# Cross attention: context halves made during self-attention and kept in DRAM; query halves split once per 128-row tile and laid over the partitions by transfers inside SBUF

## The reference, cut to what matters

```python
def _L0_xattn_ref(q, k, v, gamma):          # q is x, k and v are ctx_2048: (4, 512, 512)
    h = 8                                    # heads, each of dq = 512 // 8 = 64 rows
    qh = q.reshape(B, h, dq, Lq)
    kh = k.reshape(B, h, dq, Lk)
    vh = v.reshape(B, h, dv, Lk)
    scale = 1.0 / jnp.sqrt(jnp.asarray(dq, dtype=q.dtype))
    qk = jnp.einsum('bhdq,bhdl->bhql', qh, kh) * scale
    sm = jax.nn.softmax(qk, axis=-1)
    ret = jnp.einsum('bhql,bhdl->bhdq', sm, vh)
    return gamma * ret.reshape(B, Dv, Lq)
x = _layernorm(x + _L0_attn_ref(x, W_K, W_Q, W_V, W_O))
x = _layernorm(x + _L0_xattn_ref(x, ctx_2048, ctx_2048, gamma))
x = _layernorm(x + _L0_ffn_ref(x, W_g, W_u, W_d))
```

## Time and profile before

| | |
|---|---|
| median of 3 runs | 1504.17 us (1502.49 to 1505.21) |
| the profiled execution | 1502.57 us, of which the span is 1500.8 us |
| self-attention | from 0 to the barrier at about 992 us |
| cross attention | about 993 to 1238 us |
| feed-forward | the rest |
| busy over the span | PE 96%, DVE 73%, ACT 48%, POOL 42% |

### The profile page before, as it was taken

How to read it: one execution, slowest core, us unless ns; L and a number is a source line. 1 busy time by engine, 2 the same in 40 slices (tenths; PEclk the granted TensorE clock), 3 DMA queues, 4 the chain that set the end, 5 groups by cost and what they waited for, 6 DMA issues and landing times. The chain is left out here.

```text
span 1500.8 us, 24088 instructions
## 1 busy us (share of the span) xinstructions
PE 1434.7 (96%) x6988; PEld 1146.6 (76%) x7008; DVE 1100.5 (73%) x2368; ACT 725.1 (48%) x1549; POOL 636.6 (42%) x493
## 2 busy tenths in 40 slices
PE   7999999999999999999999999859999989999996
PEld 5788888888888888888888888737887765565564
DVE  4667677776777676777767776678999995796854
ACT  3444444545444444444353544438987863323332
POOL 1333424334243334242433433357887853343432
PEclk9999999999999999999999999979999999999998
DMA  6566666666656666666666664811224103000000
GB/s 175 155 166 169 167 169 163 167 161 166 161 164 160 161 161 171 167 165 164 162 167 158 168 166 133 210 50 54 60 60 151 36 1 112 1 29 28 0 29 28
DMA packets 193609, 185.09 MB, mean 123 GB/s; under 512 B 97057, under 2 KB 170785, under 8 KB 193313
## 3 DMA queue, kind: packets, MB, share of 16 engines
q1 hardware_dynamic: 192416, 184.09, 45.7%
q10 hardware_dynamic: 1152, 0.52, 0.2%
HBM read 113.25 MB, written 71.30 MB: 123 GB/s over the span
## 5 line engine op out<-in xcount | busy, mean ns | idle before, releaser
L583 ACT ACTIVATE probs<-probs,neg_max 128x128 f32<-128x128 f32 (+3 forms) x256 | 142.5, 557 | 357.8 <-DVE neg_max L707 350.2
L411 POOL TENSOR_TENSOR v_lo<-placed,v_hi 128x512 fp32r<-128x512 f32 x64 | 83.2, 1299 | 366.1 <-ACT v_hi L589 366.1
L413 POOL TENSOR_TENSOR pT_lo<-placed,pT_hi 128x1280 fp32r<-128x1280 f32 x64 | 189.2, 2956 | 0.0
L767 DVE SCALAR_TENSOR_TENSOR acc<-attn_bank,prob_recip,acc 128x512 f32<-128x512 f32 x256 | 174.8, 745 | 8.1 <-PE attn_bank L483 3.3
L1303 POOL TENSOR_TENSOR prod_lo<-prod,prod_hi 128x512 fp32r<-128x512 f32 x64 | 84.7, 1323 | 143.2 <-ACT prod_hi L1412 143.2
L707 DVE CUSTOM_DVE_ANT_0 probs<-attn_bank,mask 128x128 f32<-128x128 f32 (+3 forms) x256 | 117.2, 481 | 8.3
L682 DVE TENSOR_TENSOR qT_lo<-attn_bank,qT_hi 128x512 fp32r<-128x512 f32 x64 | 44.2, 691 | 105.2 <-ACT qT_hi L571 105.2
L950 POOL TENSOR_SCALAR xprobs<-xprobs,xprob_recip 128x512 f32<-128x512 f32 x128 | 99.9, 797 | 36.1 <-DVE xprob_recip L1130 36.0
L719 DVE STREAM_TRANSPOSE turned<-probs 128x256 f32<-128x256 f32 (+1 forms) x384 | 113.9, 362 | 0.0
L1362 PE MATMUL y_bank<-wdT_f32r,prod_hi 128*128 128x512 f32 x256 | 110.7, 432 | 2.3 <-POOL prod_lo L1303 1.8
L483 PE MATMUL attn_bank<-woT_hi,zT_hi 128*128 128x512 f32 x256 | 101.2, 395 | 8.9 <-DVE zT_lo L682 8.9
(11 more groups left out here) (145 smaller groups left out, 3887.5 us busy)
## 6 DMA issues: line engine op xcount, KB each, us to landing
turned_scratch<-turned SPq DMA_DIRECT2D x64, 896.0 KB, 3.9
placed<-turned_scratch SPq DMA_DIRECT2D x256, 224.0 KB, 4.3
rows_twice<-in_ctx_dram SPq DMA_DIRECT2D x64, 128.0 KB, 2.6
acc<-in_x_dram SPq DMA_DIRECT2D x16, 256.0 KB, 5.2
rows<-in_L_attn_W_V_dram SPq DMA_DIRECT2D x64, 64.0 KB, 2.3
rows<-in_L_attn_W_O_dram SPq DMA_DIRECT2D x64, 64.0 KB, 2.7
rows_twice<-in_L_ffn_W_g_dram SPq DMA_DIRECT2D x64, 64.0 KB, 3.1
rows_twice<-in_L_ffn_W_u_dram SPq DMA_DIRECT2D x64, 64.0 KB, 2.0
```

The costliest lines, as they stand in the source:

```text
L413: nc.gpsimd.tensor_tensor(pT[par][1][:], placed_probs, pT[par][0][:].bitcast(F32), ALU.subtract).then_inc(p_lo, 1)
L583: nc.scalar.activation(probs[:, cols], probs[:, cols], ACT.Exp, bias=low[:, par, t:t + 1], scale=-1.0, accum_out=total[:, par, t:t + 1]).t ...
L767: nc.vector.scalar_tensor_tensor(out=acc[:, b * NT + t, :], in0=s_bank[t][:], scalar=recip[:, b, t:t + 1], in1=acc[:, b * NT + t, :], op0= ...
```

## The change

Four things are done.

1. In self-attention, once for each of its 16 heads, SP loads one 128-row tile of the context (`load_split_tile`) into slot 1 of the buffer (now `rows_pair`), between the use of this slot for wu and the next load of wu. POOL scales it by 1/8 and splits it with three instructions (`split`), SP writes the halves (512 KB) to DRAM (`keep_halves`). The load of wu moves from the loads of b = 0 to those of b = 1, behind a wait for the split.
2. At the end of self-attention the last such split stands on POOL between the last `halves_lo` and the two `norm_gpsimd`, and SP waits for the last write before the barrier.
3. In cross attention POOL no longer splits context rows. SP loads hi and lo ready-made from DRAM straight into `cp`, as two transfers of 256 KB (`load_halves`), four items ahead instead of six, when the scores of item m + 2 are done.
4. x is split once for a pair of items: ACT rounds the whole 128-row tile (half as many instructions, of twice the partitions), POOL subtracts (one instruction per pair), and SP copies each head's hi and lo from there to the two halves of `xs` with two transfers of 128 KB inside SBUF for each item. DVE's instruction (L1136) is gone.

The diff, cut to its core:

```diff
 class ContextRows:
+    def load_split_tile(self, sp, n):
+        sp.dma_start(self.pair[:, 1, :], self.tiles[:, bass.ds(n, 1), :].rearrange("p o d -> p (o d)")).then_inc(self.split_loaded, 16)
+    def split(self, nc, pool, halves, k, n):
+        raw = self.pair[:, 1, :]
+        if not isinstance(n, int) or n > 0:
+            pool.wait_ge(self.halves_kept, n * 16)
+        wait_apart(pool, k, self.split_loaded, n * 16 + 16)
+        nc.gpsimd.tensor_scalar(raw, raw, XSCALE, 1.0, ALU.mult, ALU.mult).then_inc(self.scaled, 1)
+        wait_apart(pool, k, self.scaled, n + 1)
+        nc.gpsimd.tensor_scalar(halves[:, 0, :], raw, 1.0, 1.0, ALU.mult, ALU.mult).then_inc(self.split_hi, 1)
+        wait_apart(pool, k, self.split_hi, n + 1)
+        nc.gpsimd.tensor_tensor(halves[:, 1, :], raw, halves[:, 0, :].bitcast(F32), ALU.subtract).then_inc(self.split_done, 1)
+    def keep_halves(self, sp, halves, k, n):
+        wait_apart(sp, k, self.split_done, n + 2)
+        sp.dma_start(self.kept_tiles[:, bass.ds(n, 1), :, :].rearrange("p o k d -> p (o k) d"), halves[:].bitcast(F32)).then_inc(self.halves_kept, 16)
+    def load_halves(self, sp, cp, b, h):
+        for side in range(2):
+            sp.dma_start(cp[h % 2][side * XD:(side + 1) * XD, :, :],
+                         self.kept[bass.ds(b, 1), h * XD:(h + 1) * XD, :, :].rearrange("o r k d -> (o r) k d")).then_inc(self.halves_loaded[h % 2], 16)
...
 attention, sync: loads(h, b, more)
                     if b == 0:
                         wait_apart(sp, k, f_turn, h * 3 + 1)
                         load_gate_up(sp, "wg", h)
+                    if b == 1:
+                        wait_apart(sp, k, rows.split_done, h + 1)
                         load_gate_up(sp, "wu", h)
...
                     if b == 3:
                         keep_signs(h, 0)
+                        wait_apart(sp, k, f_turn, h * 3 + 3)
+                        rows.load_split_tile(sp, h)
...
                         keep_signs(h, 1)
                         keep_signs(h, 2)
+                        rows.keep_halves(sp, halves, k, h)
...
                 exchange(FIRST + 2, 0)
+                loads(H - 1, 1, False)
                 loads(H - 1, 2, False)
                 keep_signs(H - 1, 0)
                 exchange(FIRST + 3, 1)
+                sp.wait_ge(f_turn, (H - 1) * 3 + 3)
+                rows.load_split_tile(sp, H - 1)
...
+                rows.keep_halves(sp, halves, k, H - 1)
+                sp.wait_ge(rows.halves_kept, H * 16)
 attention, gpsimd
                 for b in range(1, B):
                     halves_lo(FIRST + b, b % 2)
+                rows.split(nc, pool, halves, k, H - 1)
                 for b in range(2):
                     norm_gpsimd(nc, pool, norm, k.minus_half, b)
 cross_attention, sync
-                    nb, nh = ahead(b, h, 6)
-                    if exists(m + 6, ITEMS) and exists(m + 4, ITEMS):
-                        wait_count(sp, cp_ready, m + 5)
-                        source.load_twice(sp, nb, nh)
+                    nb, nh = ahead(b, h, 4)
+                    if exists(m + 4, ITEMS):
+                        if exists(m + 2, ITEMS):
+                            wait_apart(sp, k, scores_full, m * NT + 3 * NT)
+                        source.load_halves(sp, cp, nb, nh)
+                        rows = slice(nh % 2 * XD, (nh % 2 + 1) * XD)
+                        if nh % 2 == 0:
+                            wait_apart(sp, k, x_lo, nb * PAIRS + (nh // 2 + 1))
+                        for part in range(2):
+                            sp.dma_start(xs[nh % 2][part * XD:(part + 1) * XD, :].bitcast(F32),
+                                         x_parts[rows, part, :]).then_inc(xs_loaded[nh % 2], 16)
                     if is_item(b, h, B - 2, 0):
                         signs.load(sp)
 cross_attention, gpsimd
-                    if exists(m + 4, ITEMS):
-                        if exists(m + 2, ITEMS):
-                            wait_apart(pool, k, scores_full, m * NT + 3 * NT)
-                        split_context(*ahead(b, h, 4))
+                    if h % 2 == 0 and exists(m + 4, ITEMS):
+                        nb, nh = ahead(b, h, 4)
+                        wait_apart(pool, k, x_hi, nb * PAIRS + (nh // 2 + 1))
+                        tile = acc[:, bass.ds(nb * NT + nh // 2, 1), :].rearrange("p o d -> p (o d)")
+                        nc.gpsimd.tensor_tensor(x_parts[:, 1, :].bitcast(F32R), tile, x_parts[:, 0, :], ALU.subtract).then_inc(x_lo, 1)
 cross_attention, tensor
                     if t == 0:
-                        pe.wait_ge(cp_ready, nb * XH + (nh + 1))
-                        pe.wait_ge(x_lo, nb * XH + (nh + 1))
+                        pe.wait_ge(source.halves_loaded[nh % 2], nb * (32 * PAIRS) + 32 * (nh // 2 + 1))
+                        pe.wait_ge(xs_loaded[nh % 2], nb * (32 * PAIRS) + 32 * (nh // 2 + 1))
 cross_attention, scalar
-                        if j == 2 and exists(m + 4, ITEMS):
+                        if j == 1 and h % 2 == 0 and exists(m + 4, ITEMS):
                             nb, nh = ahead(b, h, 4)
-                            rows = slice(nh % 2 * XD, (nh % 2 + 1) * XD)
-                            if exists(m + 2, ITEMS):
-                                act.wait_ge(scores_full, m * NT + 3 * NT)
-                            nc.scalar.activation(xs[nh % 2][rows, :], acc[rows, bass.ds(nb * NT + nh // 2, 1), :].rearrange("p o d -> p (o d)"),
-                                                 ACT.Copy, scale=XSCALE).then_inc(x_hi, 1)
+                            for i in range(2):
+                                wait_count(act, xs_loaded[i], nb * (32 * PAIRS) + 32 * (nh // 2))
+                            nc.scalar.copy(x_parts[:, 0, :].bitcast(F32R),
+                                           acc[:, bass.ds(nb * NT + nh // 2, 1), :].rearrange("p o d -> p (o d)")).then_inc(x_hi, 1)
 cross_attention, vector
-                        if j == 2 and exists(m + 4, ITEMS):
...
-                            nc.vector.scalar_tensor_tensor(out=xs[nh % 2][other, :], in0=acc[rows, bass.ds(nb * NT + nh // 2, 1), :].rearrange("p o d -> p (o d)"),
-                                                           scalar=XSCALE, in1=xs[nh % 2][rows, :].bitcast(F32),
-                                                           op0=ALU.mult, op1=ALU.subtract).then_inc(x_lo, 1)
```

More of the change, by code:

```diff
@@ L33 @@
 SCALE = 1.0 / math.sqrt(DH)
+XSCALE = 1.0 / math.sqrt(XD)
 MASKED = -1.0e10
@@ L91, in __init__ @@
         self.tiles = context.rearrange("b (t p) d -> p (b t) d", p=P)
+        self.kept = nc.dram_tensor("context_halves", (B, S, 2, D), F32).ap()
+        self.kept_tiles = self.kept.rearrange("b (t p) k d -> p (b t) k d", p=P)
         self.nat = [sb(f"rows{t}", [P, D]) for t in range(NT)]
-        self.twice = sb("rows_twice", [P, 2, D])
+        self.pair = sb("rows_pair", [P, 2, D])
         self.gamma = sb("gamma", [P, 1])
         self.nat_loaded = [sem(f"ctx_loaded{t}") for t in range(NT)]
-        self.twice_loaded = [sem(f"ctx_twice_loaded{i}") for i in range(2)]
+        self.split_loaded = sem("ctx_split_loaded")
+        self.scaled, self.split_hi, self.split_done = sem("ctx_scaled"), sem("ctx_hi"), sem("ctx_split")
+        self.halves_kept = sem("ctx_halves_kept")
+        self.halves_loaded = [sem(f"ctx_halves_loaded{i}") for i in range(2)]
         self.gamma_loaded = sem("gamma_loaded")
@@ L100, in load_tile @@
         sp.dma_start(self.nat[t][:], self.tiles[:, bass.ds(b * NT + t, 1), :].rearrange("p o d -> p (o d)")).then_inc(self.nat_loaded[t], 16)
-    def load_twice(self, sp, b, h):
-        for half in range(2):
-            sp.dma_start(self.twice[half * XD:(half + 1) * XD, h % 2, :],
-                         self.context[bass.ds(b, 1), h * XD:(h + 1) * XD, :].rearrange("o r d -> (o r) d")).then_inc(self.twice_loaded[h % 2], 16)
+    def load_split_tile(self, sp, n):
[17 more added lines that the diff above has]
+                         self.kept[bass.ds(b, 1), h * XD:(h + 1) * XD, :, :].rearrange("o r k d -> (o r) k d")).then_inc(self.halves_loaded[h % 2], 16)
     def load_gamma(self, sp):
@@ L234, in attention @@
         f_turned = sb("f_turned", [P, D])
-        raw_ffn = rows.twice
+        raw_ffn = rows.pair
+        halves = sb("ctx_halves", [P, 2, D], F32R)
         sign_gu = [sb(f"sign_{n}", [P, NC, P], BF16) for n in ("g", "u")]
@@ L382, in _ @@
                     rows.load_tile(sp, 0, t)
-                sp.wait_ge(f_turn, H * 3 + 1)
-                for h in range(2):
-                    rows.load_twice(sp, 0, h)
                 rows.load_gamma(sp)
+                rows.keep_halves(sp, halves, k, H - 1)
+                sp.wait_ge(rows.halves_kept, H * 16)
             def by_chunk(x):
@@ L427, in step @@
                         weight_lo("wq", h + 2)
+                    if b == 3:
+                        rows.split(nc, pool, halves, k, h)
                 with pool.Fori(0, H - 1) as h:
@@ L732, in _ @@
```

(9 more changed lines are left out.)

18 lines of the change are left out of this document (3 added, 15 removed).

## The result

The changed kernel takes 1511.56 us (median of 6 runs, 1509.62 to 1512.9), the kernel before 1503.76 (6 runs, 1502.32 to 1505.21). The ratio is 1.0052, with a 95% interval of 1.0039 to 1.0064: slower by some 7.8 us. My sum gave +3.7 on the profiled execution, and the forecast was 1507.1. The profiled execution took 1511.56 us, with a span of 1509.7 against 1500.8 before, so 8.9 us are to be found in the traces.

A forecast was written before the change was run, and what follows sets the result against it. PE was taken to set the pace, except at cross attention's start, items 16 to 18 and 24 to 28. +3.2 + 2.0 + 2.1 - 3.6 = +3.7 on 1502.57 gave 1506.3, raised to 1507.1; range 1500.5 to 1513.5.

The forecast's parts named there:

- the late chain: Rival in steady cross attention: query transfers land too late in each pair, 6.3 us above the sum, 1513.4; chance 0.14.
- The loop of self-attention, nothing: Self-attention's loop: POOL's 2.7 us of new instructions fit its idle time and PE never waits, so no change.
- The end of self-attention, +3.2: End of self-attention: the last split delays DVE, PE and the barrier by 2.7 us, the last exchange adds 0.5.
- The start of cross attention, +2.0: Start of cross attention: the query tile's chain delays the first score by 3.2 us, DVE's relief takes off 1.2.
- Steady cross attention, nothing: Steady pairs of cross attention: query transfers land before PE needs them and DVE's relief gains nothing, so no change.
- Items 16 to 18, +2.1: Cross attention's sign loads: item 21's transfers wait behind them and PE stalls, +2.1 us where DVE's relief alone gives -2.6.
- Items 24 to 28, -3.6: Late cross attention, where DVE is the limit: four removed instructions and faster norm work save 3.6 us.
- the signs block nothing: Rival at cross attention's sign loads: no transfer is held behind them, sum -1.0, 1502.4 us; chance 0.20.
- the query chain late in each pair: Rival in steady cross attention: SBUF transfers land in 4.3 us, PE stands 0.45 per pair, 1513.4 us; chance 0.14.
- a wait inside the loop: Rival in self-attention's loop: SP's wait or POOL's split delays each round, 1522 us at 1 us each; chance 0.04.
- DVE's relief pays in more of the stage: Rival in cross attention: DVE's relief shortens the stage by 10 us, sum -3.6, 1499.8 us; chance 0.16.
- The sign that I gave as right: Profile sign: one PE wait on a context or query transfer, 3 to 4 us, near item 18 and nowhere else.

The follow-up runs named there:

- all partitions: Changed kernel with the same context and query bytes in as many transfers, each laid over 128 SBUF partitions instead of 64: 1509.85 us, ratio 1.0040.
- Engine queries: Changed kernel with ACT and DVE making the query halves for each item as before, context halves still loaded from DRAM: 1512.67 us, ratio 1.0058.
- signs late: Changed kernel with the load of all kept signs (4 MB) moved from item 16 to item 28: 1502.83 us, ratio 0.9998.

## Why the prediction came out as it did

The places were right, two of the terms too small. The measured 1511.56 lies inside the range that I gave, but 4.5 us above the forecast of 1507.1 and just outside the 1504 to 1511 that the terms' bounds gave. What held it was the room left for rivals, the late chain above all, and that rival did not happen: that much is luck. Against the steps of the sum:

- **The loop of self-attention, nothing: right.** PE is busy 840.00 of 840.00 us, with the offset between the kernels constant within 0.03 us over 60 exchanges.
- **The end of self-attention, +3.2: right in its 2.7.** DVE waits 7.89 us instead of 5.07, 2.8 more; undoing it gave 2.7 by the ratio. From the loop's exchanges to the first transpose it is +2.6 in this trace. The 0.5 for the last exchange was not seen. Its write came 2.9 us later than before, 1.0 more than the offset that all exchanges have, yet `placed` was issued 1.97 later, just that offset. The writes' wait behind four load issues was swallowed ahead of the read. I had not counted two things of 0.8 and 0.9 that nearly cancel: the twelve matmuls after the longer wait took PE 0.8 more, at the 1.2 GHz level for all of them (before, for the first eight), and what the last exchange brought stood ready 0.9 earlier than the offset. The second is scatter, from 1.4 earlier to 0.3 later in the other executions.
- **The start of cross attention, +2.0: mis-sized, it was +4.0** in the two profiles, and +3.7 by the means of the executions with the same code (47.0 against 43.3). I priced one chain, the query tile's. Up to its last issue it ran as priced, 4.3 us behind the first transpose where my sum has 4.2. The landing took 3.9 us where I had 2.6, taken from a transfer of the same size and partitions that ran with nothing around it. At the start the queue also has 1 MB of halves, and is full (share 0.99) at 255 GB/s. So the first score came 8.3 us after the first transpose instead of 3.7: +4.6 where I had +3.2. With all partitions the same landing took 2.6 and the first score came at 7.1. The landing of 2.0 on which I put the lower bound was not seen either: of the 64 query transfers of the changed kernel none landed in under 2.2 us. "Engine queries" (7.2) shows that the halves alone would have held it nearly as long. Whether DVE's relief gave the 1.2 that I took off can't be read from a stretch that scatters by 1.6.
- **Steady cross attention, nothing: right.** The chain that I followed is the even item's, and its transfers land in 2.3 us, below the 2.6 that I took and the 3.85 from which each pair would have paid. The odd item's, behind the halves, land in 3.9, and nothing waits for them; the median of 3.0 that the view shows is of both together.
- **Items 16 to 18, +2.1: the mechanism right, the size +5.1.** The gross stall, signs late against signs where they were, is 8.0 us where I had 4.7; the relief is 2.95 where I had 2.6. The landing was 18.0 us behind the first sign issue (1156.5 - 1138.6), 15.8 in my sum. I had put 0.5 MB behind the signs at 442 GB/s, 1.2 us. Item 21's halves and queries are 0.75 MB, and they moved at 246: 3.2 us. That is 2.0 of the 2.2. The other 1.1 fit the clock, though no run separates them: after 6.55 us of waiting PE was granted 0.50, the 1.2 GHz level, in its first 3.7 us, and up to half of such a time is lost where PE is busy for all of it. That the upper bound of +5 comes so near is chance. It was to stand for the signs' 4.2 MB at half the rate, which would be 9.5 us more; and the signs did not slow down, the queue moved 393 to 451 GB/s from 1142 to 1150 us. What was slow is what stood behind them.
- **Items 24 to 28, -3.6: right.** It was -4.3, within -2.8 to -4.5. It came in four items from 26 on, 0.9 to 1.1 us each, where I had 0.7 to 0.9. By "engine queries" DVE's four removed instructions gave 3.64 of it where their own length is 2.8, and POOL's the other 0.7, where I had 0.8.

Of the rivals, "the signs block nothing" fell with the wait of 6.55 us, and "the query chain late in each pair" and "a wait inside the loop" with PE's unbroken 13.40 and 840 us. "DVE's relief pays in more of the stage" fell as well: with the signs late it is 2.95 + 4.3 us, less than 9.4. The sign that I gave as right, one wait on a transfer of 3 to 4 us near item 18, was right in its place and not in its size (6.55). Of the traces' 8.9 us against the medians' 7.8, 1.2 is that the profiled execution of before lay below its median. Put together from what repeats, the change costs 2.8 at the end of self-attention, 3.7 at the start of cross attention and 5.1 at the signs, and gives 4.3 back: +7.3, of 7.8 measured.

## What to carry to other kernels

Bytes that move from an engine into a DMA queue are free only where the queue has room at that very moment: look for the one big load that nobody waited for till now, and move it before anything urgent is queued behind it. Price a transfer by the rate of its own destination and with what is queued ahead of it, not by the landing of one that ran alone. When a wait of some us is put in front of TensorE, or shortened, compare the granted clock behind it before counting the difference as gained.

## What I had not expected of the hardware

- Transfers over 64 partitions need nearly half as much DMA share again as the same bytes over 128 (0.56 against 0.39 at 137 GB/s), and fill the queue at 246 to 255 GB/s; over 128 partitions the same queue behind the signs moves 367.
- A transfer of 128 KB from SBUF to SBUF lands only 0.3 us sooner than one from DRAM of the same shape (2.34 and 2.60 us) where nothing stands ahead of it, and no sooner behind 512 KB (3.9 both).
- Two executions with the same code at the start of cross attention differ by 1.6 us there (42.52 and 44.15), with a granted clock of 0.80 and 0.73. The three changed kernels with the earliest first score have 0.70 to 0.74 and lose 1.1 to 1.3 us of what the earlier start brought; if the one causes the other stays open.
